# Dynamic convolution: the products of the taps are added by GpSimd, from two buffers

## What is computed

```python
t   = relu(group_norm(d4_1x1(x, w1)))
wgt = einsum('oi,bighw->boghw', w2, t) + b2      # a 3 x 3 kernel for each pixel and channel group
xv  = d4_1x1(x, w_v)
pats = unfold_patches(xv, 3)                     # the 9 shifted copies of xv
out = (wv * pats).sum(axis=4)                    # wv: wgt, its taps turned for each of the 8 symmetries
```

## Time and profile before

| | before |
|---|---|
| median of 3 runs | 6316.8 us (6306.65 to 6329.6) |
| profiled execution | 6298.82 us, span 6297.0 us |
| VectorE busy | 5355.5 us, 85% |
| TensorE busy | 3268.4 us, 52% |
| ScalarE busy | 1498.1 us, 24% |
| GpSimd busy | 529.3 us, 8% |
| granted TensorE clock, mean | 0.763 |

### The profile page before, as it was taken

One profiled execution on the slowest core, in us unless ns is written; L12 is line 12 of the kernel. 1 busy time (PEld: TensorE's weight loads), 2 busy tenths in 40 slices (PEclk: granted clock), 3 DMA queues, 4 the chain that ended last, 5 costly groups with the idle time before them and its releaser, 6 DMA issues.

```text
span 6297.0 us, 42119 instructions
## 1 busy us (share of the span) xinstructions
PE 3268.4 (52%) x15026; PEld 1887.4 (30%) x15026; DVE 5355.5 (85%) x6273; ACT 1498.1 (24%) x1409; POOL 529.3 (8%) x293
## 2 busy tenths in 40 slices
PE   4442645655455465645656455465645646455345
PEld 2211323332232233223333233233323333232233
DVE  5689898888989889898898989889898888989861
ACT  1312212222132223222222231223222222231210
POOL 0000101001010010001001010010001001010000
PEclk8676777878778687877878777687877878778677
DMA  7102122231222213122231222213122121222243
GB/s 322 50 17 64 56 73 68 60 95 40 77 87 61 77 53 102 41 75 68 60 95 50 76 78 67 71 53 102 41 75 75 57 91 50 70 83 62 70 110 87
DMA packets 511491, 473.40 MB, mean 75 GB/s; under 512 B 367984, under 2 KB 449904, under 8 KB 507568
## 3 DMA queue, kind: packets, MB, share of 16 engines
q1 hardware_dynamic: 507296, 463.25, 24.1%
q0 software_dynamic: 3984, 7.45, 0.5%
HBM read 229.00 MB, written 241.57 MB: 75 GB/s over the span
## 4 chain that ended last, share of the span: by engine, by line
DVE 68%; PE 16%; ACT 6%; issue 6%; POOL 3%; DMA 1%; SPq 1%; DVEq 0%; POOLq 0%; ACTq 0%
DVE spread L1102 9%; DVE partial L1092 9%; DVE spread L1092 6%; DVE qx L764 5%; DVE work L764 5%; PE ps L475 5%; DVE work L826 4%; DVE work L817 4%; DVE partial L1109 3%; PE ps L586 3%; PE ps L645 3%; DVE partial L1108 3%; DVE stats L735 2%; PE ps L656 2%; POOL small L1355 2%
## 5 line engine op out<-in xcount | busy, mean ns | idle before, releaser
L1102 DVE TENSOR_TENSOR spread<-spread,partial 128x1344 f32<-128x1344 f32 x384 | 685.4, 1785 | 13.3
L645 PE MATMUL ps<-band,near 128*16 128x128 f32 (+1 forms) x8192 | 655.3, 489 | 79.5 <-DMA near<-img_dram 79.5
L1092 DVE TENSOR_TENSOR partial<-haty,hatx 128x1344 f32<-128x1344 f32 x384 | 679.4, 1769 | 5.5
L543 PE MATMUL ps<-work,w2x 128*128 128x512 f32 x1152 | 558.0, 614 | 161.7 <-DVE work L817 150.7
L1224 ACT ACTIVATE xp<-x,small 128x1024 f32<-128x1024 f32 x128 | 280.2, 2332 | 1401.8 <-POOL small L1355 1401.8
L645 PEld LDWEIGHTS ps<-band,near 128*16 128x16 f32 x8192 | 486.5, 127 | 294.5 <-issue 103.4
L1092 DVE TENSOR_TENSOR spread<-haty,hatx 128x1344 f32<-128x1344 f32 x288 | 458.0, 1590 | 85.7 <-ACT qx L1261 64.4
L475 PE MATMUL ps<-qx,work 128*128 128x512 f32 x512 | 277.8, 704 | 333.4 <-DVE work L843 332.7
L656 PE MATMUL ps<-samp,wout 128*128 128x256 f32 x1024 | 296.7, 441 | 283.6 <-ACT samp L1330 260.8
L817 DVE SCALAR_TENSOR_TENSOR work<-ps,cols,qx 128x512 f32<-128x512 f32 x576 | 403.2, 746 | 14.3 <-PE ps L543 5.5
L586 PE MATMUL ps<-wts,work 128*128 128x432 f32 x512 | 223.0, 601 | 369.1 <-ACT work L1305 369.1
(11 more groups left out here) (229 smaller groups left out, 5262.5 us busy)
## 6 DMA issues: line engine op xcount, KB each, us to landing
band<-taps_dram SPq DMA_DIRECT2D x512, 288.0 KB
taps_dram<-partial SPq DMA_DIRECT2D x832, 72.0 KB, 2.1
near<-img_dram SPq DMA_DIRECT2D x256, 128.0 KB
img_dram<-band SPq DMA_DIRECT2D x6, 4096.0 KB, 40.9
om_now<-om SPq DMA_DIRECT2D x32, 576.0 KB, 5.2
om_dram<-om SPq DMA_DIRECT2D x32, 576.0 KB, 6.0
taps_dram<-partial SPq DMA_DIRECT2D x320, 54.0 KB, 2.1
x<-x_in SPq DMA_DIRECT2D x16, 1024.0 KB, 10.4
```

Of the source, the lines that this page charges most:

```text
L543: pe.matmul(bank(4 + i % 4), w2x[:, half, tap, :], tr[:, h * HALF:(h + 1) * HALF], start=True, stop=True).then_inc(s_w, 1)
L645: mm = pe.matmul(o, near[:, j, g * CG:(g + 1) * CG], band[:, :, a:z, j * G + g], start=False, stop=(j == JB - 1), skip_group_check=True)
L1092: return build(vec.tensor_tensor(o, haty[:, :, 3 * i:3 * i + 3, :].rearrange("p e j a -> p j e a"), cells, ALU.mult))
L1102: done = build(vec.tensor_tensor(skew, skew, spare, ALU.add))
```

## The change

In dyn GpSimd does the sixteen adds of a batch. VectorE writes the products of a tap alternately into two buffers, `tmp` and the first 1024 elements of `big`, and waits before it writes one until the add that read it has ended (semaphore `s_added`). GpSimd waits for the second multiply of a tap and for its own last add. The addition into x waits for the last add. In `BUILD_AT` two places are new, dyn + 6.5 and dyn + 8.5, and two are gone, pw + 2 and ln + 3. There are 18 rows as before, taken in the same order, so rows 9 and 10 stand in dyn now, and rows 11 to 15 each stand one or two places further forward than they did: row 11 at L2 + 3.5 (it was row 9's place), row 12 at pw + 1 (row 10's), row 13 at L3 + 3.5, row 14 at the start of ln, row 15 at ln + 2.

```diff
-    + [STEP["L2"] + 3.5, STEP["pw"] + 1, STEP["pw"] + 2, STEP["L3"] + 3.5, STEP["ln"], STEP["ln"] + 2, STEP["ln"] + 3,
+    + [STEP["dyn"] + 6.5, STEP["dyn"] + 8.5, STEP["L2"] + 3.5, STEP["pw"] + 1, STEP["L3"] + 3.5, STEP["ln"], STEP["ln"] + 2,
        STEP["om"] - 0.1, STEP["om"] + 4]
...
+        products = (work[:, 3 * N:4 * N], big[:, 0:4, :].rearrange("p t n -> p (t n)"))
...
-                summed = 0
+                adds = f * K * (TAPS - 1)
                 for i in range(K * TAPS * 2):
                     half, tap, h = i // (2 * TAPS), i // 2 % TAPS, i % 2
                     if i % 4 == 0:
                         yield STEP["dyn"] + i // 4 + 1
-                    wait(ve, s_v, summed)
                     ve.wait_ge(s_w, f * 2 * K * TAPS + i + 1)
                     o = acc[:, half, h * HALF:(h + 1) * HALF]
-                    t = o if tap == 0 else tmp[:, h, :]
+                    if tap > 0:
+                        wait(ve, s_added, adds + half * (TAPS - 1) + tap - len(products))
+                    t = o if tap == 0 else products[tap % 2][:, h * HALF:(h + 1) * HALF]
                     vec.scalar_tensor_tensor(
...
-                    if h == 1 and tap > 0:
-                        ve.wait_ge(s_wu, f * 2 * K * TAPS + i + 1)
-                        o = acc[:, half, :]
-                        chain[0] += 1
-                        summed = chain[0]
-                        vec.tensor_tensor(o, o, work[:, 3 * N:4 * N], ALU.add).then_inc(s_v, 1)
                 yield STEP["dyn"] + 10
-                ve.wait_ge(s_v, summed)
+                ve.wait_ge(s_added, adds + K * (TAPS - 1))
                 link(vec.tensor_tensor(xflat, xflat, work[:, 0:K * N], ALU.add))
...
+                for half in range(K):
+                    for tap in range(1, TAPS):
+                        i = half * 2 * TAPS + 2 * tap + 1
+                        yield STEP["dyn"] + i // 4 + 1.1
+                        po.wait_ge(s_wu, f * 2 * K * TAPS + i + 1)
+                        added = f * K * (TAPS - 1) + half * (TAPS - 1) + tap - 1
+                        wait(po, s_added, added)
+                        pool.tensor_tensor(acc[:, half, :], acc[:, half, :], products[tap % 2], ALU.add).then_inc(s_added, 1)
```

More of the change, by code:

```diff
@@ L229, in build @@
         s_xvz = sem("s_xv_border_zeroed")
+        s_added = sem("s_tap_products_added")
         s_dw0 = sem("s_depthwise_first_tap")
```

## The result

The median went from 6321.15 us (6306.65 to 6329.6, four runs) to 6262.01 us (6255.36 to 6267.81, four runs; the table of the kernel before has three of its four runs): ratio 0.9908, 95% interval 0.9886 to 0.9931. That is 59 us, where 120 were forecast. The profiled execution after took 6259.87 us with a span of 6258.1; against the profile before its span is 38.9 us shorter. That is less than the 59 because the execution profiled before lay 22 us under its median and the one after 2 us.

What follows compares the result with a forecast made beforehand. VectorE, busy 85% of the span, was taken as the bound. Saving 7.4 us in each of 15 batches plus 8.6 in the first, 120 us, gave 6179 profiled, 6197 as median; range 6105 to 6340.

Steps and rivals of the forecast that it cites:

- A: Period of GpSimd's adds in dyn: forecast 2.2 us, bounds 2.0 and 2.7; nothing gained at 2.66.
- table add: GpSimd's add of two constant tables, 1152 elements in 2.11 us, one operand still: price 1.66 ns per element.
- 19.7 + 16A: Length of dyn with rows 9 and 10: 19.7 us outside the add periods plus sixteen periods, 54.9 us.
- order of the turns in rows 9 and 10: In dyn: row 9's hat product before add 10, then its other instructions; row 10's first product before add 14.
- empty buffers after each: In dyn, after rows 9 and 10 both product buffers are empty: 1.5 us each for a multiply pair.
- cover in pw: In pw, the remaining full row just covers VectorE's wait for ScalarE: ends 3116.8 against 3116.68, margin 0.1 us.
- L2 was taken as even: In L2, a full row replaces row 9 with its hat product: no gain counted, 1.7 us either way.
- PE's clock: In dyn's two rows the clock may fall, but four filled banks cover two taps: counted at nothing.
- Multiplies exclude adds too: Rival in dyn: GpSimd's reads block PSUM multiplies, nothing overlaps, 75.0 us a stage, 204 us slower, 6521; chance 0.15.
- The add costs the upper bound: Rival in dyn: A = 2.7, stage 63.2 us, 0.9 lost each batch, about 6330; chance 0.10.
- Rows and adds overlap: Rival in dyn: adds pending at rows are hidden, stage 49.0 us, 13.3 us a batch gained, 6108; chance 0.07.
- The cover is missed: Rival in pw and ln: VectorE waits for ScalarE 4 to 7 us a batch, 6290 to 6330; chance 0.08.

Runs made afterwards that it cites:

- run with a still operand: Changed kernel, each GpSimd add's second operand 8 products each held for 128 elements: add 1.90 us, dyn 51.5 us, program 12409 us with a different sum.
- adds alone: Kernel before with GpSimd doing the adds from two buffers, all rows of tap weights at their old places: ratio 0.9906 to the kernel before, median 6249.29 us.
- rows alone: Kernel before with rows 9 and 10 moved into dyn, adds still on VectorE: ratio 0.9970, 6299.26 us.
- drained run: Changed kernel, but VectorE waits before rows 9 and 10 until GpSimd has done all adds handed over: dyn 59.3 to 59.6 us, one execution 6272.32 us.
- three buffers: Changed kernel with three product buffers in place of two: ratio 0.9897 to the kernel before, 6238.71 us, dyn 57.7 us.
- halves in order: Kernel before, rows unmoved, GpSimd adding 512 pixels after VectorE adds the other 512 of each tap: ratio 0.9782, median 6166.87 us, dyn 37.6 us.
- same halves started earlier: The halved adds in order, but GpSimd starts each tap after its first multiply: dyn 44.6 us, one execution 6277.13 us.

## Why the prediction was wrong

**The step that failed: the price of an add.** The forecast took A, the time from one add of GpSimd to the next, as 2.2 us: 2.1 for the add, "near the add since it is an add, and a little above it", and 0.08 for the gap, between bounds of 2.0 and 2.7. It is 2.50: the add takes 2.36 where 2.1 was taken, the gap 0.13 where 0.08 was read. In the sixteen adds of a batch that is 4.8 us, 77 us in all, more than the whole miss of 61 (120 forecast, 59 measured). The turns gave 22 us of it back, and waits for ScalarE in pw took 5 (both below): 77 - 22 + 5 = 60. The run with a still operand shows why the add was priced too low. The table add was cheap because one of its operands stands still: in the same place of the kernel an add costs 1.90 us that way and 2.36 with both operands moving. The text named this difference and then gave it 0.2 us. From 512 elements in 1.28 us and 1024 in 2.36 an element costs 2.11 ns, and 0.2 us are fixed. The Trainium skill (GPSIMD Engine Reference, Performance versus the Vector engine) has 4497 ns for 2048 elements; half of that, an estimate of 2.25 us, was nearer than the row. Its factor of 1.96 between the engines is 1.9 here (2.36 against 1.23 us).

**The rest of the stage's account was right.** The formula was 19.7 + 16A. With A = 2.50 it gives 59.7; measured are 58.2. The 1.5 us are at the turns: an instruction that waited for its turn ends sooner behind the other's end than its length and the gap say, 2.2 us for the adds 10 and 14 in place of 2.5, 4.2 for the hat product in place of 4.35, 1.4 for the products in place of 1.56, and behind adds 9, 13 and 16 no gap to a next add is paid. The order of the turns in rows 9 and 10, the empty buffers after each (GpSimd idle 4.53 and 6.17 us, the row's tail and one pair of 1.49) and GpSimd as pace maker all stand in the timeline as forecast.

**The moved rows.** ln gave back 9.5 us as predicted and pw 6.1 (6.3 predicted): the margin of 0.1 us that the forecast gave the cover in pw was missed in nine batches, by 5.2 us in all. L2 was taken as even. The change shows 23.4 us from the addition into x to the depthwise taps against 22.5 before, mean of thirteen batches. But the six kernels with row 11 there show 21.4 to 23.5, the four with row 9 22.1 to 23.3, so I count it as scatter of single executions. What stretches rows there can be seen in the trace before: the 955 products and sums of 1344 elements with no sampling matmul (L645) beside them take 1.53 to 1.60 us, the 101 with some beside them 3.3 on average and up to 8.6. That the matmuls are the cause isn't shown. The two parts together give less than apart: adds alone 3.8 us a batch, rows alone 1.9 (dyn + 13.6, given back 15.5), both 46.6 + 15.5 - 58.2 = 3.9. Beside GpSimd's adds the rows lengthen dyn by 15.4 us (42.8 to 58.2), just what they give back, since the pair of multiplies behind each row, 1.49 us, has no add to lie beside. The forecast's sums had this, 8.6 us for a batch without the rows and 7.4 with them, and its text didn't say that the moved rows bring nothing. PE's clock, counted at nothing, shows in the windows after row 9 (length, busy of PE, PEld, DVE, ACT and POOL, granted clock):

```profile
3019.00:3029.00 10.00, 1.32 (x4) 0.25 (x2) 9.90 (x4) 0.00 (x0) 7.05 (x2) 0.73 0.00 0
3029.00:3033.00 4.00, 2.96 (x4) 1.42 (x5) 2.92 (x5) 0.00 (x0) 2.28 (x1) 0.50 0.29 74
```

PE had filled its banks and stood still; the clock fell to 0.50, the 1.2 GHz level. VectorE then waited once for PE where it would have waited for GpSimd. Its waits for PE before the multiplies are 11.9 us in all, 5.5 before the change, so the effect is next to nothing.

**The rivals.** *Multiplies exclude adds too*: refuted, multiplies stay at 0.745 us beside adds of 2.36 and adds beside them cost 0.02 more than the stage's last one (2.34). The Trainium skill (SBUF — State Buffer, Who interferes with whom) says that a VectorE instruction with one SBUF input doesn't contend with GpSimd, and these traces agree. *The add costs the upper bound*: half true, A went 60% of the way from 2.2 to 2.7 (with A = 2.7 the formula gives 62.9 us, not the 63.2 stated). *Rows and adds overlap*: refuted by the drained run and three buffers. *The cover is missed*: it was, in pw, but by 5.2 us in all, where the rival needs 4 to 7 in each batch. The range held the time (6262 in 6105 to 6340) and the sign was right; the size was forecast at twice what came.

## What to carry to other kernels

Price an operation on an engine from a row with the same form of operands: an operand that stands still is not a cheap sample of a moving one, and in a lockstep of sixteen the difference is paid sixteen times. Where two engines take turns by whole instructions, moving work between them saves only what can lie beside work that needs no turn, here the multiplies from PSUM. Cut the moved share to just that window and order it behind the other engine's turn: halves in order gave 2.2% and the whole add 0.9%; the same halves started earlier lost 7.0 us a stage against halves in order.

## What was not expected of the hardware

GpSimd's float32 add of two tensors in SBUF took 1.90 us for 128 x 1024 with an operand that holds each element 128 times, 2.36 with both moving, and 1.28 for 128 x 512. An instruction that has to wait for its turn is recorded from its issue on (an add of 6.27 us, a product of 3.69), and it ends about 0.15 us sooner behind the other's end than its plain length (2.20 against 2.36, 1.41 against 1.56).
